# Routing inside a linear-attention and expert block: keys and queries of four groups as two ScalarE parts added by GpSimd, ten groups of base moves on ScalarE, and TensorE's third group ahead of the class counts

## The chip, the cores and the metric

One core of one Trainium2 chip. The metric is the device time of one execution in microseconds (us). TensorE is PE in the profile, VectorE DVE, ScalarE ACT, GpSimd POOL, and SP the queue that starts most transfers.

## What is computed

`x` is (8, 1024, 128). `xn` is its layer norm. The result is `x + attention(xn) + ffn(xn)`, and ffn returns `xn` plus the expert part.

```python
# linear attention, B=8, T=1024, D=128
xn = layer_norm(x, ln_g, ln_b)
q, k, v = split(xn @ qkv_w + qkv_b)
k = k * sigmoid(xn @ gate_w + gate_b)
q = elu(q) + 1.0
k = elu(k) + 1.0
attn = einsum('btd,bsd->bts', q, k) * tril
out = einsum('bts,bsd->btd', attn, v) / (sum(q * cumsum(k)) + DEN_EPS)
# experts, E=8, FF=256, K=2
scores = (x @ router_w.T + router_b) / temp
gates = sinkhorn(scores, iters=3)
topk_vals, topk_idx = top_k(gates, 2)
g = relu(x @ wg[e]);  p = x @ wp[e];  y = (g * p) @ wo[e]
result = x + weighted sum of the two chosen experts
```

## The kernel before, in words

The 8192 tokens are 64 tiles of 128, in 16 groups of four tiles; two groups are one sequence of the batch. Each engine has one instruction stream, written out by hand, and counts on semaphores order them. Nothing is scheduled by a program: an engine does its list in order, and a wait holds all that stands behind it.

Stage one (to about 42 us): statistics, normalised rows, their transposes `zT`, and for each group the logits and values `lv`. At the same time SP clears two scratch arrays in HBM, `by_lower` and `by_upper`.

Stage two, the routing with the first groups of the attention (42 to about 90 us). VectorE runs the Sinkhorn rounds over all tokens: `spread_maxima`, `shift_columns` (then a second exponential on ScalarE, L726, `rB<-rA`), `weigh_rows` (L1019), column sums on TensorE (`route_sums`, L1524), `column_factors` (L1024), `row_factors`, three times; then `first_best`, `second_best` (from L1045), `members` (the last, L1057, makes the class membership), `tile_sums`, `class_bounds`, `slots` (L1084 writes `placed`, the step PLACED). TensorE counts in `route_counts`, `route_totals` and `route_places`. Between these stand the steps of groups 0 to 3. GpSimd meanwhile moves the base rows of all 16 groups (L522: `rows = rows * r1p + base_off`, 64 operations), and then prepares the gates (from L534).

A group n of the attention takes these steps:

- TensorE `project(n, "g")`, `"k"`, `"q"` (L1453): 128x512 products for the gate, the key and the query.
- ScalarE `tanh_gate` (L678), VectorE `gate_key` (L935, tile `kg`), ScalarE `exp_key` (L690, `ek`) and `relu_key` (L693, `rk`), VectorE `key` (L946): `kp = min(ek, 1) + rk`.
- ScalarE `exp_query` (L684, `eq`), VectorE `query` (L941): `qp = max(min(eq, 1), q)` with q read from PSUM.
- TensorE `score(n)` (L1571), VectorE `mask(n)` (L959); TensorE `turn_key(n)` (L1579), ScalarE `save_kt` (L699, `ktok`).
- TensorE `add_state` (L1507) and ScalarE `save_state` (L709) in turn for four tiles; TensorE `out_chunk` (L1491, L1494).
- VectorE `finish(n)` (L965 to L973): divides and adds to the base row. It waits for the base move of its group.

`score(3)` waits for the step PLACED, since the places and the scores share a PSUM bank. On TensorE 34 small filler products (L1620) stand before the counts.

Stage three (to about 170 us): groups 3 to 15 in a loop over `range(EARLY, NG)`, with `EARLY = 3`; GpSimd scatters finished rows to `by_lower` (L557), once the slots are known. ScalarE also splits expert weights after some groups (`round_expert`, L713). Stage four: two passes of 41 entries over the experts, TensorE nearly always busy.

The key and the query on VectorE before are:

```python
def key(n):
    dve.wait_ge(ek_done, n + 1)
    dve.scalar_tensor_tensor(kp[:, n % 2].rearrange("p g t -> p (g t)"), ek[:], 1.0, rk[:],
                             ALU.min, ALU.add).then_inc(kp_done, 1)
```

## Time and profile before

| | us |
|---|---|
| median of 3 runs | 378.62 (378.27 to 380.6) |
| the profiled execution | 379.69 |
| its span in the profile | 376.5 |
| TensorE busy / VectorE busy in the span | 338.0 / 267.9 |
| GpSimd busy / ScalarE busy | 267.7 / 235.8 |

The span is the time between the first and the last instruction that the profiler saw; the rest lies around it. Busy times overlap and can't be added. A timeline row gives the start, the length, the engine, the line, and in square brackets the idle time ahead of it and what ended it.

### The profile page before, as it was taken

What the parts mean: (1) busy time and instruction counts of PE and PEld (TensorE: products, weight loads), DVE (VectorE), ACT (ScalarE), POOL (GpSimd) and SP (SyncE); (2) the same over time, 40 slices, a digit from 0 to 9 for tenths busy, and PEclk for the clock granted to TensorE, in tenths of its full rate; (3) what the DMA queues carried; (4) which work ended last, traced back from release to release, by engine and by line L of the source; (5) the groups of instructions that cost most, each with busy time, mean ns of one, the idle gap of its engine ahead of it and who ended that gap; (6) DMA issues with size and microseconds to landing.
All of it is one profiled execution on the core that took longest, in us unless ns stands there. A gap on an engine that the chain in (4) does not pass through costs nothing.

```text
span 376.5 us, 8784 instructions
## 1 busy us (share of the span) xinstructions
PE 338.0 (90%) x2584; PEld 307.0 (82%) x2584; DVE 267.9 (71%) x733; ACT 235.8 (63%) x442; POOL 267.7 (71%) x363
## 2 busy tenths in 40 slices
PE   0889799889999999988699999999899999999780
PEld 0769568667888887878699999999899999999670
DVE  3998889998888888776545677666666667666440
ACT  3689744225776766657445877777587777775430
POOL 3686999947777756566377677777737777777773
PEclk9999999979999999999989999999999999999996
DMA  6999999998424413248965776776664555553330
GB/s 180 286 326 334 336 334 262 305 265 252 142 103 141 157 71 128 90 140 219 317 209 173 189 220 195 214 219 193 179 172 131 162 143 136 169 150 103 110 87 0
DMA packets 64284, 70.96 MB, mean 188 GB/s; under 512 B 6098, under 2 KB 59102, under 8 KB 64240
## 3 DMA queue, kind: packets, MB, share of 16 engines
q1 hardware_dynamic: 54112, 48.70, 48.8%
q0 software_dynamic: 8672, 21.19, 15.6%
q10 hardware_dynamic: 1456, 0.53, 0.7%
q8 instruction: 22, 0.36, 0.4%
q14 instruction: 22, 0.18, 0.2%
HBM read 28.54 MB, written 43.04 MB: 190 GB/s over the span
## 4 chain that ended last, share of the span: by engine, by line
PE 64%; DVE 13%; DMA 10%; issue 4%; POOL 4%; ACT 2%; SPq 0%; ACTq 0%; DVEq 0%; POOLq 0%
PE psum L1698 13%; PE psum L1683 7%; PE psum L1685 7%; PE psum L1684 7%; PE psum L1507 4%; PE psum L1571 4%; PE psum L1659 3%; DMA row<-by_lower 3%; POOL out L587 3%; PE psum L1400 3%; DVE stats L876 3%; PE psum L1453 2%; PE psum L1491 2%; DMA rows<-in_L_attn_x 2%; DMA by_lower<-rows,slot_u 2%
## 5 line engine op out<-in xcount | busy, mean ns | idle before, releaser
L573 POOL DMA_INDIRECT by_upper<-row x70 | 69.1, 987 | 30.1 <-issue 20.5
L587 POOL DMA_INDIRECT out<-row x70 | 68.9, 985 | 25.9 <-issue 16.5
L557 POOL DMA_INDIRECT by_lower<-rows,slot_u x64 | 63.9, 998 | 30.6 <-issue 17.9
L1698 PE MATMUL psum<-w_expert,hT 128*128 x560 | 77.0, 277 | 0.8 <-DVE hT L1333 0.5
L1683 PE MATMUL psum<-xT_high,w_now 128*128 128x256 f32 x232 | 70.6, 305 | 1.9 <-DVE xT_low L1324 1.1
L1698 PEld LDWEIGHTS psum<-w_expert,hT 128*128 128x128 f32 x560 | 69.7, 192 | 1.5 <-issue 1.1
L788 ACT ACTIVATE w_now<-w_split 128x1024 fp32r x58 | 61.4, 1058 | 14.1 <-PE psum L1685 13.6
L1685 PE MATMUL psum<-xT_high,w_now 128*128 128x256 f32 x232 | 65.7, 283 | 0.0
L1684 PE MATMUL psum<-xT_low,w_now 128*128 128x256 f32 x232 | 65.3, 282 | 0.0
L1337 DVE TENSOR_TENSOR hT<-relu,psum 128x512 f32<-128x512 f32 x58 | 39.9, 688 | 34.7 <-PE psum L1685 30.9
L1345 DVE SCALAR_TENSOR_TENSOR row<-psum,row 128x128 f32<-128x128 f32 x140 | 43.7, 346 | 9.7 <-PE psum L1698 2.8
L807 ACT ACTIVATE relu<-psum 128x512 f32<-128x512 f32 x58 | 34.7, 598 | 20.1 <-PE psum L1685 19.7
L1683 PEld LDWEIGHTS psum<-xT_high,w_now 128*128 128x128 f32 x232 | 44.4, 191 | 2.5 <-ACT w_now L788 1.3
L1684 PEld LDWEIGHTS psum<-xT_low,w_now 128*128 128x128 f32 x232 | 44.4, 191 | 0.0
L1685 PEld LDWEIGHTS psum<-xT_high,w_now 128*128 128x128 f32 x232 | 44.1, 190 | 0.0
L522 POOL TENSOR_SCALAR rows<-rows,r1p,base_off 128x128 f32<-128x128 f32 x64 | 35.1, 564 | 0.1
L1659 PE MATMUL psum<-ident,row 128*128 128x128 f32 x140 | 28.9, 276 | 6.8 <-DMA row<-by_lower 3.6
L1324 DVE TENSOR_TENSOR xT_low<-psum,xT_high 128x256 fp32r<-128x256 f32 x58 | 24.5, 425 | 8.0 <-ACT xT_high L797 4.4
L1507 PEld LDWEIGHTS psum<-lv,ktok 128*128 128x128 f32 x112 | 17.8, 190 | 14.8 <-ACT ktok L699 7.7
L1507 PE MATMUL psum<-lv,ktok 128*128 128x129 f32 x112 | 26.0, 314 | 1.9 <-ACT state L709 0.9
L1673 PE MATMUL psum<-xT_plain,w_plain 128*128 128x128 f32 x192 | 25.4, 275 | 0.0
L1659 PEld LDWEIGHTS psum<-ident,row 128*128 128x128 f32 x140 | 17.9, 142 | 8.3 <-DMA row<-by_lower 4.0
(265 smaller groups left out, 688.0 us busy)
## 6 DMA issues: line engine op xcount, KB each, us to landing
by_lower<-blank SPq DMA_DIRECT2D x1, 10140.0 KB, 34.6
by_upper<-blank SPq DMA_DIRECT2D x1, 10062.0 KB, 71.3
row<-by_lower SPq DMA_DIRECT2D x29, 260.0 KB, 3.6
row<-by_upper SPq DMA_DIRECT2D x29, 258.0 KB, 2.9
rows<-in_L_attn_x SPq DMA_DIRECT2D x8, 512.0 KB, 9.2
row<-by_lower SPq DMA_DIRECT2D x12, 130.0 KB, 3.2
row<-by_upper SPq DMA_DIRECT2D x12, 129.0 KB, 2.2
by_upper<-row POOLq DMA_INDIRECT x70
```

The costliest lines, as they stand in the source:

```text
L557: pool.indirect_dma_start(by_lower, bass.IndirectOffsetOnAxis(ap=slot_u[:, t:t + 1], axis=0), rows[:, t, :], None)\
L573: pool.indirect_dma_start(by_upper, bass.IndirectOffsetOnAxis(ap=row[:, q, k, SLOT_UP:SLOT_UP + 1].bitcast(U32), axis=0), row[:, q, k, 0:R ...
L587: pool.indirect_dma_start(out_rows, bass.IndirectOffsetOnAxis(ap=row[:, q, k, TOKEN:TOKEN + 1].bitcast(U32), axis=0), row[:, q, k, BASE], ...
L788: act.activation(w_now[:, n % 2, :], w_split[:, bass.ds(number, 1), 0:4 * FF].rearrange("p a f -> p (a f)"), ACT.Copy).then_inc(w_copied, 1)
L1337: dve.tensor_tensor(hT[:, n % 3].rearrange("p f t -> p (f t)"), relu[:, n % 2], psum[:, 2 * (n % 2) + 1, :], ALU.mult).then_inc(h_done, 1)
L1345: dve.scalar_tensor_tensor(target, psum[:, 4 + n % 2, k * D:(k + 1) * D], row[:, n % NB, k, by:by + 1], target, ALU.mult, ALU.add)\
L1507: pe.matmul(psum[:, 5, 0:D1], ktok[:, c, :], lv[:, n * G + c, V1], start=(cb == 0), stop=True, skip_group_check=True).then_inc(s_ready, 1)
L1659: last = pe.transpose(psum[:, 6 + n % 2, k * P:(k + 1) * P], row[:, n % NB, k, Z], ident[:])
L1683: pe.matmul(target, high, x_high, start=True, stop=False)
L1684: pe.matmul(target, high, x_low, start=False, stop=False)
L1685: last = pe.matmul(target, low, x_high, start=False, stop=True)
L1698: last = pe.matmul(psum[:, 4 + n % 2, k * D:(k + 1) * D], hT[:, n % 3, f, k * P:(k + 1) * P], weights, start=(f == 0), stop=(f == FB - 1))
```

## The change

Four things change.

- Keys and queries of groups 0 to 3 (`ON_POOL = EARLY + 1`) are no longer made by VectorE. ScalarE makes two parts: `relu(-x)`, `relu(x)` and then `exp(-relu(-x))` of the first; GpSimd adds the two. For the query a new tile `rq` holds the second part. A key takes three ScalarE operations instead of two, a query three instead of one. A semaphore `below` makes the exponential wait for its own input. Groups from 4 on stay as they were.
- Base moves: GpSimd keeps groups 5 to 10, interleaved with its keys and queries. ScalarE takes ten: 0 to 4 among its early steps, and 11 to 15 after groups 5, 7, 9, 11 and 12 (`LATE_BASE`). `base_done` becomes `base_act` and `base_pool`, and `finish` waits for the one that counts its group.
- VectorE's order: keys and queries leave it; `gate_key(2)` moves ahead of `weigh_rows(2)`; `mask(2)`, `gate_key(3)` and `finish(1)` move between the best and the second-best expert; `finish(2)` comes before the slots.
- TensorE's order: the outputs of group 2, the query of group 3 and the gate of group 4 move ahead of the counts, and the 34 filler products go.

The diff, cut to its core:

```diff
+        ON_POOL = EARLY + 1
+        ACT_BASE, POOL_BASE = (0, 1, 2, 3, 4, 11, 12, 13, 14, 15), (5, 6, 7, 8, 9, 10)
...
+        LATE_BASE = {5: 11, 7: 12, 9: 13, 11: 14, 12: 15}
...
-            for n in range(NG):
+
+            def move_base(n):
                 for t in range(n * G, (n + 1) * G):
                     last = pool.tensor_scalar(rows[:, t, BASE], rows[:, t, BASE], r1p[:, t:t + 1],
                                               base_off[:, t:t + 1], ALU.mult, ALU.add)
-                last.then_inc(base_done, 1)
+                last.then_inc(base_pool, 1)
+
+            def query(n):
+                pool.wait_ge(eq_done, n + 1)
+                if n >= 2:
+                    pool.wait_ge(o_ready, n - 1)
+                pool.tensor_tensor(qp[:, n % 2].rearrange("p g t -> p (g t)"), eq[:], rq[:], ALU.add).then_inc(qp_done, 1)
+
+            def key(n):
+                pool.wait_ge(ek_done, n + 1)
+                pool.tensor_tensor(kp[:, n % 2].rearrange("p g t -> p (g t)"), ek[:], rk[:], ALU.add).then_inc(kp_done, 1)
+
+            move_base(5)
+            move_base(6)
+            move_base(7)
+            key(0)
+            query(0)
+            move_base(8)
+            key(1)
+            query(1)
+            move_base(9)
+            key(2)
+            query(2)
+            move_base(10)
+            key(3)
+            query(3)
...
+                if n < ON_POOL:
+                    act.activation(eq[:], psum[:, bank_q(n), :], ACT.Relu, bias=ones[:, 0:1], scale=-1.0).then_inc(below, 1)
+                    act.activation(rq[:], psum[:, bank_q(n), :], ACT.Relu, bias=minus_one[:])
+                    act.wait_ge(below, 2 * n + 2)
+                    act.activation(eq[:], eq[:], ACT.Exp, scale=-1.0).then_inc(eq_done, 1)
+                    return
...
+                if n < ON_POOL:
+                    act.activation(ek[:], kg[:], ACT.Relu, scale=-1.0).then_inc(below, 1)
+                    act.activation(rk[:], kg[:], ACT.Relu)
+                    act.wait_ge(below, 2 * n + 1)
+                    act.activation(ek[:], ek[:], ACT.Exp, scale=-1.0).then_inc(ek_done, 1)
+                    return
...
+                for t in range(n * G, (n + 1) * G):
+                    last = act.activation(rows[:, t, BASE], rows[:, t, BASE], ACT.Identity, bias=base_off[:, t:t + 1],
+                                          scale=r1p[:, t:t + 1])
+                last.then_inc(base_act, 1)
...
+                if n in LATE_BASE:
+                    move_base(LATE_BASE[n])
...
             for n in range(EARLY, NG):
-                finish(n - 1)
+                if n > EARLY:
+                    finish(n - 1)
...
             for n in range(EARLY, NG):
                 ahead = n + 1 < NG
-                if ahead:
+                if ahead and n > EARLY:
                     project(n + 1, "g")
```

Lines of the changed kernel are numbered anew: L726 is L782 there, L1045 is L1110, L1453 is L1512, L1571 is L1630, L1507 is L1566, L1491 and L1494 are L1550 and L1553.

ScalarE, from the first exponential of the routing to the saved key of group 0. Before (`rB<-rA` are the two exponentials, `ek` and `rk` the key's parts, `eq` the query's, `th` the gate):

```order
L721 ACTIVATE rB<-rA 128x512
L690 ACTIVATE ek<-kg 128x512
L693 ACTIVATE rk<-kg 128x512
L684 ACTIVATE eq<-psum,minus_one 128x512
L726 ACTIVATE rB<-rA 128x512
L678 ACTIVATE th<-psum 128x512
L729 ACTIVATE w_high<-w_in 128x384
L690 ACTIVATE ek<-kg 128x512
L693 ACTIVATE rk<-kg 128x512
L684 ACTIVATE eq<-psum,minus_one 128x512
L699 ACTIVATE ktok<-psum 128x512
```

The same place now (the `rows` operations are base moves):

```order
L727 ACTIVATE ek<-kg 128x512
L728 ACTIVATE rk<-kg 128x512
L730 ACTIVATE ek<-ek 128x512
L715 ACTIVATE eq<-psum,ones 128x512
L716 ACTIVATE rq<-psum,minus_one 128x512
L718 ACTIVATE eq<-eq 128x512
L770 ACTIVATE rows<-rows,base_off,r1p 128x128 x4
L782 ACTIVATE rB<-rA 128x512
L708 ACTIVATE th<-psum 128x512
L785 ACTIVATE w_high<-w_in 128x384
```

Between the two exponentials there stood three operations, now ten; between the second one and the saved key the same again, with base move 1 in it.

VectorE now, around the second-best expert (`scores` is the mask of group 2, `kg` the gated key of group 3, `den` to `rows` the finish of group 1, `rA<-rank,score` the start of the second best):

```order
L1103 TENSOR_REDUCE score<-best_h 128x64
L1018 TENSOR_TENSOR scores<-psum,causal 128x512
L994 SCALAR_TENSOR_TENSOR kg<-th,psum 128x512
L1030 TENSOR_SCALAR den<-psum 128x4
L1033 RECIPROCAL rden<-den 128x4
L1038 SCALAR_TENSOR_TENSOR rows<-psum,rden,rows 128x128 x4
L1110 TENSOR_TENSOR rA<-rank,score 128x512
```

Before, the mask and the gated key stood behind the members, and query 3 and the reciprocal of the gates behind the finish:

```order
L1057 TENSOR_TENSOR member<-cls,class_no 128x896
L959 TENSOR_TENSOR scores<-psum,causal 128x512
L1064 CAST tile_sum<-psum 64x14
L935 SCALAR_TENSOR_TENSOR kg<-th,psum 128x512
```

The mask of group 2 and the gated key of group 3 have moved ahead of the second best, and with them the finish of group 1.

## Rows read from the trace of the kernel before

**Rows 1.** The page, busy time by engine: us, share of the span, instructions

```profile
PE 338.0 (90%) x2584; PEld 307.0 (82%) x2584; DVE 267.9 (71%) x733; ACT 235.8 (63%) x442; POOL 267.7 (71%) x363
```

**Rows 2.** Busy time of each engine by stretch, granted clock, DMA

```profile
core 0: us, PE busy (x) PEld busy (x) DVE busy (x) ACT busy (x) POOL busy (x), PEclk, DMA share, GB/s
...
60.00:70.00 10.00, 8.93 (x65) 7.48 (x64) 9.62 (x20) 4.04 (x9) 10.00 (x18) 1.00 1.07 251
...
80.00:90.00 10.00, 10.00 (x47) 7.36 (x45) 8.65 (x25) 2.49 (x6) 5.30 (x9) 0.68 1.09 275
```

**Rows 3.** Timeline of TensorE, scores of groups 3, 4 and 5

```profile
86.03 1.24 PE L1571 MATMUL psum<-qp,kp 128*128 128x128 f32 x8
...
93.05 1.16 PE L1571 MATMUL psum<-qp,kp 128*128 128x128 f32 x8
...
99.78 1.05 PE L1571 MATMUL psum<-qp,kp 128*128 128x128 f32 x8
```

**Rows 4.** Timeline of ScalarE: four normalised tiles; key 0, query 0, second exponential

```profile
13.26 1.64 ACT L620 ACTIVATE rows<-rows,z_off,rs 128x128 f32<-128x128 f32 x4
...
45.22 0.63 ACT L690 ACTIVATE ek<-kg 128x512 f32<-128x512 f32 x1 [0.48 <-DVE kg L935]
...
45.76 0.61 ACT L693 ACTIVATE rk<-kg 128x512 f32<-128x512 f32 x1
...
46.41 0.69 ACT L684 ACTIVATE eq<-psum,minus_one 128x512 f32<-128x512 f32 x1
...
48.28 0.63 ACT L726 ACTIVATE rB<-rA 128x512 f32<-128x512 f32 x1 [1.19 <-DVE rA L1013]
```

**Rows 5.** Timeline of GpSimd and VectorE where both work on 128x64 or 128x384

```profile
23.38 1.00 POOL L487 TENSOR_TENSOR w_in<-w_in,w_sum 128x384 f32<-128x384 f32 x1
...
73.78 0.72 POOL L534 TENSOR_TENSOR rC<-rC 128x256 f32<-128x256 f32 x1
73.91 0.64 DVE L1055 TENSOR_SCALAR cls<-v 128x64 f32<-128x64 f32 x1
74.47 0.18 DVE L1056 TENSOR_SCALAR cls<-u 128x64 f32<-128x64 f32 x1
...
74.69 1.24 DVE L1057 TENSOR_TENSOR member<-cls,class_no 128x896 bf16<-128x896 f32 x1
75.06 1.04 POOL L536 TENSOR_TENSOR score<-score 128x64 f32<-128x64 f32 x1
```

**Rows 6.** Timeline: first row weights, column sums of rounds 1 and 2, third column factors

```profile
48.94 0.69 DVE L1019 TENSOR_TENSOR rC<-rB,u 128x512 f32<-128x512 f32 x1
...
55.33 2.00 PE L1524 MATMUL psum<-rC,ones 128*128 128x64 f32 x16
...
61.20 1.90 PE L1524 MATMUL psum<-rC,ones 128*128 128x64 f32 x16
...
63.72 0.55 DVE L1024 RECIPROCAL v<-psum 128x64 f32<-128x64 f32 x1
```

**Rows 7.** Timeline of TensorE: query of group 2, last output product of group 1

```profile
63.38 1.88 PE L1453 MATMUL psum<-zT,w_in 128*128 128x512 f32 x4
...
67.97 0.39 PE L1494 MATMUL psum<-state,qp 128*128 128x129 f32 x2
```

**Rows 8.** Timeline of VectorE: second best, mask of group 2, places

```profile
69.11 0.68 DVE L1045 TENSOR_TENSOR rA<-rank,score 128x512 f32<-128x512 f32 x1
...
75.96 0.69 DVE L959 TENSOR_TENSOR scores<-psum,causal 128x512 f32<-128x512 f32 x1
...
80.83 1.97 DVE L1084 TENSOR_TENSOR placed<-psum,member 128x448 f32<-128x448 f32 x2
```

**Rows 9.** Timeline of ScalarE, group 5 in the loop

```profile
106.22 0.60 ACT L678 ACTIVATE th<-psum 128x512 f32<-128x512 f32 x1 [0.81 <-PE psum L1456]
107.89 0.60 ACT L699 ACTIVATE ktok<-psum 128x512 f32<-128x512 f32 x1 [1.07 <-PE psum L1579]
```

**Rows 10.** GpSimd's waits: engine, line, waited for, us in total, times, longest

```profile
POOL by_lower L557 <- DVE rows L973: 12.3, 12, 2.0
```

**Rows 11.** Busy time by engine and granted clock in one us

```profile
85.00:86.00 1.00, 1.00 (x2) 0.34 (x1) 0.93 (x6) 0.00 (x0) 0.69 (x1) 0.50 1.14 262
```

More of the change, by code:

```diff
@@ L241, in sparse_block_kernel @@
             eq = first("eq", [P, GW])
+            rq = first("rq", [P, GW])
             kp = first("kp", [P, 2, G, P])
@@ L261, in sparse_block_kernel @@
             "rw_loaded rw_pe rw_step w_scaled w_summed w_sum_saved w_step")
-        (stat_step, var_ready, sqrt_out, scale_ready, z_act, z_dve, z_pool, zT_ready, zT_act, zT_dve, base_done) = steps(
-            "stat_step var_ready sqrt_out scale_ready z_act z_dve z_pool zT_ready zT_act zT_dve base_done")
+        (stat_step, var_ready, sqrt_out, scale_ready, z_act, z_dve, z_pool, zT_ready, zT_act, zT_dve, base_act, base_pool, below) = steps(
+            "stat_step var_ready sqrt_out scale_ready z_act z_dve z_pool zT_ready zT_act zT_dve base_act base_pool below")
         lv_ready = [sem(f"lv_ready{g}") for g in range(NG)]
@@ L717, in round_z, with move_base @@
                 act.activation(z_high(n), group(n), ACT.Copy).then_inc(z_rounded, 1)
+            def move_base(n):
+                if n == 0:
+                    act.wait_ge(scale_ready, len(BLOCKS) + 1)
+                    act.wait_ge(z_act, len(ACT_Z))
+                    act.wait_ge(z_dve, len(DVE_Z))
+                    act.wait_ge(z_pool, len(POOL_Z))
+                for t in range(n * G, (n + 1) * G):
+                    last = act.activation(rows[:, t, BASE], rows[:, t, BASE], ACT.Identity, bias=base_off[:, t:t + 1],
+                                          scale=r1p[:, t:t + 1])
+                last.then_inc(base_act, 1)
             tanh_gate(0)
@@ L739, in _ @@
             exp_key(2)
-            relu_key(2)
             save_kt(1)
@@ L746, in _ @@
             save_state(1, 2)
+            move_base(3)
+            exp_key(3)
             save_kt(2)
@@ L960, in mask, with wait_base @@
                                   causal[:].unsqueeze(1).to_broadcast([P, G, P]), ALU.mult).then_inc(a_masked, 1)
+            def wait_base(n):
+                if n in ACT_BASE:
+                    dve.wait_ge(base_act, ACT_BASE.index(n) + 1)
+                else:
+                    dve.wait_ge(base_pool, POOL_BASE.index(n) + 1)
             def finish(n):
@@ L1136, in _ @@
             shift_columns()
-            query(0)
             weigh_rows(0)
-            key(0)
             gate_key(1)
@@ L1144, in _ @@
             mask(0)
-            query(1)
-            key(1)
             column_factors(1)
             row_factors()
+            gate_key(2)
             weigh_rows(2)
-            gate_key(2)
             mask(1)
@@ L1154, in _ @@
             first_best()
-            query(2)
-            key(2)
+            mask(2)
+            gate_key(3)
+            finish(1)
             second_best()
             members()
-            mask(2)
             tile_sums()
-            gate_key(3)
             class_bounds()
-            finish(1)
-            query(3)
+            finish(2)
             invert_gates()
             slots()
-            key(3)
             def pair_bounds():
@@ L1617, in _ @@
             add_state(2, 1)
+            out_chunk(2, 0)
+            out_chunk(2, 1)
+            project(3, "q")
             add_state(2, 2)
-            for _ in range(34):
-                pe.matmul(psum[:, ROUTE_BANK, 0:P], before_h[:], before_h[:], start=True, stop=True)
+            out_chunk(2, 2)
+            add_state(2, 3)
+            out_chunk(2, 3)
+            project(4, "g")
             route_counts()
             route_totals()
-            project(3, "q")
             route_places()
-            add_state(2, 3)
-            for c in range(G):
-                out_chunk(2, c)
             for n in range(EARLY, NG):
                 ahead = n + 1 < NG
-                if ahead:
+                if ahead and n > EARLY:
                     project(n + 1, "g")
```

15 lines of the change are left out of this document (9 added, 6 removed).

## The prediction, made before the changed kernel ran

> **What bounds the kernel now.** I began with the share of time by engine: TensorE is busy 90% of the span and VectorE 71% [rows 1], an average over stages with different limits. So I cut the span into stretches [rows 2]. From 60 to 70 us VectorE is busy 96%, from 80 to 90 us 87%, TensorE's weight loads 75 and 74% and ScalarE 40 and 25%: this is the routing, from 42 to 85 us, one long chain on VectorE (exponential, three rounds of row and column factors, best and second-best expert, classes, places), and the first four groups of the linear attention are woven into it. From 100 us on the groups run alone at an even pace: their scores start at 86.03, 93.05 and 99.78, 6.7 us apart [rows 3]. Each group depends on the states of the last, and the expert stage needs the last rows, so whatever moves the score of group 4 (93.05) moves everything behind it. All groups from 4 on keep their instructions; only five groups' base moves on ScalarE are new there. So the whole question is when the score of group 4 starts.
>
> The profiled execution took 379.69 us: 376.5 of span and 3.2 around it. The median of the runs is 378.62. I work out a difference in the trace and add it to the median.
>
> **The step units.** ScalarE: the two passes over the key start 0.54 apart (45.22, 45.76), and a pass that reads PSUM with a bias takes 0.69, about 0.60 from start to start; a 128x128 pass with scale and bias costs 1.64 for four, that is 0.385 each and 1.54 for a group [rows 4]. So a key in parts takes 3 x 0.54 = 1.62 where it took 1.08, a query 0.60 + 0.60 + 0.54 = 1.74 where it took 0.60. Four groups: 4 x (0.54 + 1.14) = 6.7 us more, and ten base moves 15.4 us, five of them (7.7 us) before group 3. GpSimd: the addition of two 128x512 tensors isn't in the trace. The nearest row is 1.00 for 128x384, the same operation [rows 5]: from below 1.0, from above 1.0 x 512/384 = 1.33 plus what a neighbour on VectorE may add (1.7); I take 1.35. VectorE loses eight operations of 0.69, which start 0.60 apart: 4.8 us.
>
> **The change, leg by leg**, against the trace of before. A time of the new kernel is a sum of row durations along its written order.
>
> 1. *To the first row weights.* The second exponential ran at 48.28 on ScalarE, as soon as VectorE had its input [rows 4]. Now it stands behind key 0 (45.22 + 1.62), query 0 (+ 1.74) and base move 0 (+ 1.54): 50.1. The first row weights, at 48.94 before, start at 50.75: **+1.8**. Before, VectorE's query 0 ran beside the exponential; nothing covers the wait now.
>
> 2. *To the second column sums.* TensorE's column sums of round 1 are queued behind the first state product, which needs the saved key of group 0. On ScalarE that save is now behind gate 1, key 1 (from 52.3, 1.62), base move 1 (1.54), query 1 (1.74): it ends at 57.8, and the sums start at 58.0 where they started at 55.33 [rows 6]: +2.6 in all, **+0.8** on this leg. That VectorE reaches the same place at 57.3 or, if GpSimd's additions don't hold it, at 56.2, changes nothing: ScalarE is late.
>
> 3. *To the third column factors.* Sums end 60.1; reciprocal, factors, sum and reciprocal 2.6; the gate of key 2 is now written ahead of the row weights (0.60); weights 0.70 and sums 2.0: the factors of round 3 start at 66.1. Before it was 63.72, where the sums were done at 63.1 and waited for VectorE's mask and finish [rows 6]: +2.4 in all, **-0.2**. Removing queries and keys from VectorE pays here, little.
>
> 4. *To the second-best expert.* This is the worst place. The best expert takes 4.0 us, to 70.1. Then the mask of group 2 is written, which needs its scores. Before, TensorE began that group's query at 63.38 and was through its queue (last product of group 1 at 67.97, 0.22 to the next) at 68.2 [rows 7], 4.8 us later; the mask stood 7 us further down VectorE's order (75.96) and never waited. Now the query's product starts after the third sums and four transposes, at 66.35; 4.8 more and 0.8 for states that ScalarE saves only after the three parts of query 2 and gate 3: scores start 72.0, are out at 73.2. VectorE stands still 3.1 us. Gate 3 then waits for its key product, which is behind scores (0.89), transposes (0.46) and its own 1.05: 74.4, another 0.6. Mask and gate 1.2, finish of group 1 1.45. Second best starts at 76.5, where it was 69.11 [rows 8]: +7.4 in all, **+5.0**.
>
> 5. *Second best and class members.* 69.11 to 75.93 before, 6.8. The same operations now run beside key 3 and query 3 on GpSimd. What that costs: a 128x64 step on the class numbers took 0.64 beside GpSimd's addition and ended with it (74.55 and 74.50), the next one took 0.18; and GpSimd's 128x64 product beside the member test took 1.04, as long as 128x384 elsewhere [rows 5]. So the two hold each other up. Between 0 and 1.9 us (two additions of 1.35, less the part before VectorE comes); I take **+1.3**.
>
> 6. *Members to places.* 75.93 to 82.80 before. The chain is counts 0.64, copy, totals, bounds 0.8, places, a reciprocal, two products of 0.97. Mask, gate and query have left it and the finish of group 2 has come in; 6.65 against 6.87: **-0.2**. Places are known at 91.3.
>
> 7. *Places to the scores of group 3.* Here is the gain. Before, the products of group 2's output, the gate product of group 4 and key 3 came after: the scores started 3.2 us behind the places, at 86.03. Now all that is done, and the scores start at once: **-3.2**.
>
> 8. *Group 3.* 7.02 us before. One finish (1.45) has left VectorE, but slot sums, casts and pair bounds now follow the places there: 7.2, **+0.2**.
>
> Sum: 1.8 + 0.8 - 0.2 + 5.0 + 1.3 - 0.2 - 3.2 + 0.2 = +5.5. Scores of group 4 at 98.5.
>
> **What is hidden.** The five late base moves (1.54 each) are in groups without an expert split or with a free stretch: in group 5 (from 106 us) ScalarE waits 0.81 before the gate and 1.07 behind it [rows 9], 1.88 in all for 1.54. They cost nothing; uncovered they would cost 5 x 1.54 = 7.7 us. GpSimd's scatters start some 7.6 us later but the rows only 5.5; it waited 12.3 us in all for rows [rows 10], and 2.1 us of that go, so it still catches up before the last group. The expert stage is untouched.
>
> **A rule weighed.** The rows above show GpSimd and VectorE holding each other up [rows 5]. The Trainium skill, "SBUF — State Buffer" (SBUF: two separate sides), says that the two share a port pair as "an **exclusive lock**, not a bandwidth split", taken by an operation of VectorE with two SBUF inputs against a GpSimd operation that reads SBUF. The trace agrees in both pairs of leg 5. By the rule in full, leg 5 is +1.9, without it 0: a total of +6.1 or +4.2.
>
> **The rivals.**
> *A, the clock.* TensorE's granted clock averages 0.68 from 80 to 90 us [rows 2] and stands at 0.50, its level of 1.2 GHz, at 85 [rows 11], after a stretch with waits for the members; the 34 filler products are gone now, and TensorE is idle from 74.4 to 77.4 and for much of 84 to 91. If the half clock comes later and reaches into group 3 (it doubles some 3 to 4 us of products there and in the places), the total is +8 to +9: 387. For it: the stalls of leg 4. Against: more products stand before the counts. Chance 0.2.
> *B, half of it.* ScalarE's and TensorE's delays overlap better: no hold-up by GpSimd (-1.3), scores of group 2 not behind the states (-0.8), the half clock, which lay on the path of legs 6 and 7, gone (-1): +2.4, 381. Chance 0.2.
> *C, faster.* VectorE was 87 to 96% busy [rows 2]: if the chain stays bound by it and GpSimd and ScalarE keep ahead, eight operations (4.8) leave it and leg 7 comes in full with 3.2, less 1.8 of leg 1 and the 1.3 of leg 5: -4.9, 373.7. Its place is the mask of group 2: it decides if scores 2 are out by 70.1, that is 3.1 us sooner than worked out. Against: leg 2 by ScalarE's queue alone. Chance 0.13.
>
> **How the numbers follow.** The forecast (legs as above, +4 to +7) has 0.47. Predicted 378.62 + 5.5 = 384.1 us. The range runs from B's low end, 379.5, to A's 388; outside lie C and a few hundredths. Slower by over 1% (3.8 us, about what a measurement of this kernel tells from no change) is the forecast, A and a little of B: 0.69; within 1%: most of B, 0.18; faster: C, 0.13.
>
> **What would show it.** In the profile after: the second exponential at 50, sums of round 1 at 58, VectorE idle before the mask of group 2 by about 3 us with TensorE's scores as the releaser, second best at 76 to 77, the scores of group 3 right behind the places near 91, group 4 at 98 to 99, then 6.7 a group. If the mask of group 2 doesn't wait, leg 4 and the sign are wrong; if the scores of group 4 come later than 100, look at the granted clock from 80 to 98; if the pace after group 4 isn't 6.7, the late base moves weren't hidden.

## The result, and the profile after

| | before | after |
|---|---|---|
| median of 4 runs, us | 378.96 (378.27 to 380.6) | 385.36 (381.94 to 386.64) |
| profiled execution / its span | 379.69 / 376.5 | 384.35 / 382.6 |
| start of the second exponential | 48.28 | 50.00 |
| second-best expert starts | 69.11 | 76.28 |
| class members known / places known | 75.93 / 82.80 | 83.24 / 91.97 |
| scores of group 3 / group 4 | 86.03 / 93.05 | 92.23 / 101.90 |

The changed kernel is slower: ratio 1.017, with a 95% interval from 1.0121 to 1.022. The forecast was 384.1 us, a difference of 5.5 where 6.4 was measured. The sign and the place are right. Three terms of the sum are not: together they put the scores of group 4 at 8.85 us late instead of 5.5, and part of that comes back at the end of the kernel.

The page of after, busy time by engine, answers to [rows 1]:

```profile
PE 337.8 (88%) x2550; PEld 306.7 (80%) x2550; DVE 263.3 (69%) x725; ACT 256.0 (67%) x494; POOL 254.8 (67%) x331
```

VectorE has lost 4.6 us of work and GpSimd 12.9, ScalarE has gained 20.2. VectorE was the busiest engine of the routing, and the kernel is slower all the same. The waits of VectorE say why. View: waits of VectorE in after, 50 to 100 us (what waited, what it waited for, us in total, times, longest):

```profile
DVE scores L1018 <- PE psum L1630: 4.1, 2, 3.1
DVE tile_sum L1129 <- PE psum L1591: 2.8, 1, 2.8
DVE v L1089 <- PE psum L1583: 2.8, 2, 1.4
DVE rC L1084 <- ACT rB L782: 2.6, 1, 2.6
```

Each line is a wait: 2.6 us for the second exponential, 3.1 for the scores of group 2, 2.8 for the counts. The 4.6 us that VectorE no longer works it waits, and more. The same three places in the timeline of VectorE in after (start, length, line, idle time ahead and its releaser):

```profile
50.73 0.69 DVE L1084 TENSOR_TENSOR rC<-rB,u 128x512 f32<-128x512 f32 x1 [2.59 <-ACT rB L782]
...
72.94 0.69 DVE L1018 TENSOR_TENSOR scores<-psum,causal 128x512 f32<-128x512 f32 x1 [3.13 <-PE psum L1630]
74.23 0.69 DVE L994 SCALAR_TENSOR_TENSOR kg<-th,psum 128x512 f32<-128x512 f32 x1 [0.60 <-PE psum L1512]
...
76.28 0.68 DVE L1110 TENSOR_TENSOR rA<-rank,score 128x512 f32<-128x512 f32 x1
...
86.08 0.16 DVE L1129 CAST tile_sum<-psum 64x14 bf16<-64x14 f32 x1 [2.84 <-PE psum L1591]
```

They answer to [rows 6] and [rows 8]. TensorE's granted clock is the last piece. View: TensorE by stretches of 2 us in after (stretch, us, busy us and count, granted clock, DMA share, GB/s):

```profile
78.00:80.00 2.00, 1.99 (x9) 0.50 1.11 243
80.00:82.00 2.00, 2.00 (x9) 0.68 1.10 262
82.00:84.00 2.00, 0.63 (x6) 1.00 1.14 246
...
86.00:88.00 2.00, 0.78 (x10) 1.00 1.01 315
88.00:90.00 2.00, 1.98 (x13) 0.53 0.40 123
90.00:92.00 2.00, 0.00 (x0) 0.50 0.03 11
92.00:94.00 2.00, 1.77 (x8) 0.50 0.00 0
94.00:96.00 2.00, 2.00 (x8) 0.50 0.00 0
96.00:98.00 2.00, 2.00 (x5) 0.50 0.37 133
98.00:100.00 2.00, 2.00 (x14) 0.92 0.19 67
```

The clock is at 0.50, its level of 1.2 GHz, from 78 to about 81 and again from 88 to 98 us, the second time right through group 3. TensorE had stood idle for 3.02 us up to 77.15 before the first fall, and was busy only 0.63 us from 82 to 84 and 0.78 from 86 to 88 before the second.

### The profile page after: what moved, and what is told of

The parts are those of the page before. It is cut to its first block, busy times and chain, and to the rows that moved or that the text cites. A ratio compares the mean times of both kernels' runs of the same rounds, so it can differ in the third digit from the quotient of the medians.

```text
span 382.6 us, 8732 instructions
## 1 busy us (share of the span) xinstructions
PE 337.8 (88%) x2550; PEld 306.7 (80%) x2550; DVE 263.3 (69%) x725; ACT 256.0 (67%) x494; POOL 254.8 (67%) x331
## 4 chain that ended last, share of the span: by engine, by line
PE 69%; DVE 8%; ACT 6%; DMA 6%; issue 5%; POOL 4%; SPq 0%; ACTq 0%; DVEq 0%; POOLq 0%
PE psum L1758 14%; PE psum L1743 7%; PE psum L1745 7%; PE psum L1744 7%; PE psum L1566 5%; PE psum L1630 4%; PE psum L1733 4%; PE psum L1719 4%; POOL out L617 3%; PE psum L1459 3%; PE psum L1550 2%; PE psum L1512 2%; DVE stats L935 2%; PE psum L1553 2%; DMA rows<-in_L_attn_x 2%
## 5 line engine op out<-in xcount | busy, mean ns | idle before, releaser
L587 POOL DMA_INDIRECT by_lower<-rows,slot_u x64 | 65.0, 1015 | 29.4 <-issue 18.5
L1566 PEld LDWEIGHTS psum<-lv,ktok 128*128 128x128 f32 x112 | 18.5, 195 | 22.1 <-ACT ktok L743 11.8
L1566 PE MATMUL psum<-lv,ktok 128*128 128x129 f32 x112 | 26.1, 315 | 7.8 <-ACT ktok L743 4.8
L1550 PE MATMUL psum<-lv,scores 128*128 128x129 f32 x128 | 24.0, 280 | 0.0
```

What stands on the lines that cost most here:

```text
L587: pool.indirect_dma_start(by_lower, bass.IndirectOffsetOnAxis(ap=slot_u[:, t:t + 1], axis=0), rows[:, t, :], None)\
L1566: pe.matmul(psum[:, 5, 0:D1], ktok[:, c, :], lv[:, n * G + c, V1], start=(cb == 0), stop=True, skip_group_check=True).then_inc(s_ready, 1)
```

## The experiments

The start of the routing moves by 2 us between executions. So from here on a point is counted from the column shift, one VectorE operation that stands ahead of all that changes (47.56 in before, 47.45 in after, 46.2 to 48.3 in the others). All in us behind it:

| kernel | first row weights | column sums, round 1 | second best | members | places | scores 3 | scores 4 | ratio to before, 95% |
|---|---|---|---|---|---|---|---|---|
| before | 1.38 | 7.77 | 21.55 | 28.37 | 35.24 | 38.47 | 45.49 | 1 |
| after | 3.28 | 10.51 | 28.83 | 35.79 | 44.52 | 44.78 | 54.45 | 1.017, 1.012 to 1.022 |
| x1 | 1.74 | 9.87 | 28.64 | 36.56 | 43.63 | 43.88 | 52.99 | 1.016, 1.010 to 1.023 |
| x2 | 3.28 | 14.11 | 32.43 | 39.39 | 48.55 | 48.81 | 56.18 | 1.022, 1.017 to 1.028 |
| x3 | 3.28 | 13.10 | 31.41 | 39.33 | 45.71 | 46.61 | 53.38 | 1.013, 1.006 to 1.021 |
| x4 | 3.28 | 13.68 | 25.56 | 32.12 | 45.60 | 45.86 | 55.25 | 1.028, 1.024 to 1.033 |
| x5 | 3.29 | 10.53 | 28.85 | 35.81 | 44.34 | 44.60 | 53.91 | 1.020, 1.014 to 1.026 |
| x6 | 3.28 | 10.52 | 28.83 | 36.74 | 45.51 | 46.15 | 54.25 | 1.020, 1.012 to 1.028 |
| x7 | 3.27 | 10.52 | 22.40 | 29.60 | 36.97 | 37.61 | 45.57 | 0.996, 0.992 to 1.001 |
| x8 | 1.39 | 7.77 | 21.54 | 28.35 | 35.66 | 35.92 | 44.10 | 0.998, 0.994 to 1.001 |
| x9 | 3.29 | 14.11 | 25.99 | 33.19 | 40.57 | 41.20 | 49.17 | 1.000, 0.995 to 1.005 |
| x10 | 1.75 | 9.57 | 21.46 | 28.66 | 36.05 | 36.67 | 44.62 | 0.989, 0.983 to 0.996 |
| x11 | 3.28 | 10.53 | 28.84 | 35.51 | 43.80 | 46.40 | 53.12 | 1.015, 1.010 to 1.021 |
| x12 | 1.75 | 9.57 | 21.46 | 28.66 | 36.05 | 36.67 | 44.63 | 0.995, 0.990 to 1.001 |

Read the table by differences in a row, not only by its last time. Each row is one profiled execution; where the clock is the same, a step repeats to a few hundredths. The ratio is against the kernel before in the same job. Filler products compute nothing that is used: they only keep TensorE busy.

### x1: early base moves back on GpSimd

```diff
-        ACT_BASE, POOL_BASE = (0, 1, 2, 3, 4, 11, 12, 13, 14, 15), (5, 6, 7, 8, 9, 10)
+        ACT_BASE, POOL_BASE = (11, 12, 13, 14, 15), tuple(range(11))
```

> The changed kernel with base moves 0 to 4 on GpSimd (as before the change) instead of ScalarE, the late ones 11 to 15 still on ScalarE. Theory Q (each leg is set by a queue, and the loss at the second-best expert is by the keys and queries in parts): the second exponential comes 1.5 us earlier (48.5 instead of 50.0), the row weights of round 1 at 49.2, the column sums of round 1 at about 56 instead of 57.96; but GpSimd now has the moves ahead of its additions, the scores of group 2 come hardly earlier (71 to 72), second best at 75 to 76.5, scores of group 4 at 100 to 102: total 383.5 to 386, within 1% of the changed kernel. Rival S (ScalarE's five early base moves, 7.7 us, carry the loss): scores of group 4 at 96 or before, total 379 to 380.

Median 384.68. The row weights come 1.54 us sooner, one base move exactly, but the column sums only 0.64, and second best 0.19. So the five early moves (7.7 us of ScalarE's time) aren't the loss. (At the scores of group 4 this profile is 1.46 us ahead of after; in the ratio nothing of it shows.) Leg 1 was won and lost again at the next wait: the key product of group 1 waited 1.58 us for GpSimd's query 0, and gate 1 waited 0.84 for it.

### x2: the counts ahead of two states

```diff
             project(3, "q")
+            route_counts()
+            route_totals()
             add_state(2, 2)
...
-            project(4, "g")
-            route_counts()
-            route_totals()
             route_places()
+            project(4, "g")
```

> The changed kernel with TensorE's class counts and totals written behind query 3's product, ahead of the states (2,2), (2,3) and their outputs, and the gate product of group 4 behind the places. Theory Q (in the changed kernel the counts, at 85.37, stand in TensorE's queue behind states that ScalarE saves only after query 3 in three parts): the counts start right behind the tile sums' copy, at 82.9 to 83.5, the idle time of 2.84 before the tile sum on VectorE falls to about 1, places known at 89.5 to 90.5 instead of 91.97; the gate product of group 4 then stands between places and scores 3 and takes 0.9 to 1.7 back: scores 3 at 91 to 92, scores 4 at 100.5 to 101.9, total 383.5 to 385.5. Rival C (only the half clock, which products in the queue merely stretch, matters): the places come at 91.5 or later, as the same products fall into the same stretch at 0.50.

The counts started 0.06 us behind the members (86.45 against 86.39) where after needs 2.13, as theory Q has it. But from members to places it took 9.16 us, no less than after's 8.73: TensorE ran at 0.50 from 80 to 96 us, and states, outputs and places stretched. So up to the places the new order pays nothing while the clock is down. Behind them it does: from scores 3 to scores 4 it took 7.37 us instead of 9.67, the clock being back at 1.00 from about 97 us, and from the second best to scores 4 it took 23.75 instead of 25.62. Both expectations of this run hold in half. And a new thing shows: the clock was at 0.50 already at 50 us, and the column sums came at 14.11 instead of 10.51. These 3.6 us hide the gain in the time.

### x3: 119 fillers in the tail

```diff
+            pe.wait_ge(a_masked, 3)
+            keep_warm(50, ROUTE_BANK)
             add_state(2, 0)
...
+            keep_warm(20, 3)
             add_state(2, 3)
...
             route_totals()
+            keep_warm(15, 3)
             route_places()
+            keep_warm(34, 3)
```

> The changed kernel with 119 filler products on TensorE, in its idle stretches of the routing's tail: 50 behind the masked scores of group 2 (74 to 77 us), 20 and 15 about the counts, 34 behind the places' product. They compute nothing that is used. Theory C (the half clock from 78 to 98 costs 2.5 us in group 3 and 0.5 to 1 before the places): granted clock near 1.0 from 78 to 98, places at 91 to 91.5, scores 3 to scores 4 in 7.0 to 7.3 us instead of 9.67, scores 4 at 98 to 99, total 381 to 382.5. Rival W (group 3 is long because slot sums, casts and bounds on VectorE stand in its way, whatever the clock): the clock rises but scores 3 to scores 4 stays at 9 us or more, total 384 to 386.

View: TensorE in x3, by 2 us, about the counts and the places (members at 87.11, places at 93.49):

```profile
84.00:86.00 2.00, 1.74 (x21) 1.00 1.06 319
86.00:88.00 2.00, 1.39 (x16) 1.00 0.51 157
88.00:90.00 2.00, 1.90 (x26) 1.00 0.08 19
90.00:92.00 2.00, 2.00 (x16) 0.57 0.00 0
92.00:94.00 2.00, 2.00 (x24) 0.58 0.00 0
94.00:96.00 2.00, 2.00 (x23) 1.00 0.00 0
```

Scores 3 to scores 4 took 6.77 us instead of 9.67, members to places 6.38 instead of 8.73. Rival W is out: the missed part of leg 8 is the clock. The fillers cost 0.6 of it back, since the last 34, partly at half clock, ended 0.9 us behind the places.

TensorE's order is that of after here, and still the counts start 0.06 us behind the members. View: timelines of GpSimd, VectorE and TensorE in x3:

```profile
84.84 1.32 POOL L535 TENSOR_TENSOR qp<-eq,rq 128x512 f32<-128x512 f32 x1 [3.84 <-ACT eq L718]
85.07 2.04 DVE L1122 TENSOR_TENSOR member<-cls,class_no 128x896 bf16<-128x896 f32 x1
87.17 0.60 PE L1591 MATMUL psum<-ones_h,member 128*64 128x1 bf16 x14 [0.39 <-DVE member L1122]
```

Of that, 0.95 us is the members themselves, which end later (2.04 us beside GpSimd's query 3 instead of 1.09). The rest of after's 2.13 is the same queue run through at the full clock. From the second best to scores 4 it took 21.97 us instead of 25.62, so holding the clock up in the tail is worth 3.65, and it pays alone. The median is 383.30, but the ratio, 1.013 against 1.017, has an interval that overlaps after's: the early fall of the clock was in this profile too, with 2.59 us at the column sums.

### x4: the tail's orders as before

The orders of VectorE, TensorE and ScalarE from the second-best expert on are those of before; keys, queries and base moves stay where the change put them.

```diff
-            mask(2)
-            gate_key(3)
-            finish(1)
             second_best()
             members()
+            mask(2)
             tile_sums()
+            gate_key(3)
             class_bounds()
-            finish(2)
+            finish(1)
```

> The changed kernel, keys and queries still in three ScalarE parts added by GpSimd and base moves on ScalarE, but the orders of VectorE, TensorE (with its 34 filler products) and ScalarE from the second-best expert on as in the kernel before. Theory Q: the mask of group 2 no longer stands ahead of the second-best expert, which starts at 70.5 to 72 instead of 76.28; the class members end at 76 to 77.5 instead of 83.24; the price comes later: key 3 and query 3 on GpSimd and the outputs of group 2 behind the places, scores 4 at 97 to 100, total 379 to 383, between the two kernels. Rival P (the parts and GpSimd's additions are themselves too slow, wherever the mask stands): second best starts no earlier than 74 or the members' steps beside GpSimd take over 8 us, scores 4 at 101.5 or later, total 385 or more.

The slowest of all, 388.32. Second best came 3.27 us sooner than in after although the column sums were 3.17 later: 6.44 in all, the two waits for scores and key product (3.13 and 0.60) and the work of mask, gate and finish. And then it was thrown away. View: VectorE's timeline in x4, ahead of the places:

```profile
84.14 1.13 DVE L1038 SCALAR_TENSOR_TENSOR rows<-psum,rden,rows 128x128 f32<-128x128 f32 x4
91.03 0.55 DVE L1144 RECIPROCAL score<-score 128x64 f32<-128x64 f32 x1 [5.76 <-POOL score L571]
91.50 1.90 DVE L1149 TENSOR_TENSOR placed<-psum,member 128x448 f32<-128x448 f32 x2
```

VectorE stood 5.76 us for GpSimd's gate sums. View: GpSimd in x4:

```profile
84.82 1.27 POOL L539 TENSOR_TENSOR kp<-ek,rk 128x512 f32<-128x512 f32 x1 [7.87 <-ACT ek L730]
86.48 1.27 POOL L535 TENSOR_TENSOR qp<-eq,rq 128x512 f32<-128x512 f32 x1 [0.40 <-ACT eq L718]
87.71 0.73 POOL L564 TENSOR_TENSOR rC<-rC 128x256 f32<-128x256 f32 x1
```

GpSimd had waited 7.87 us for key 3 with the gates queued behind it, and their input was ready at 78.3. I had expected 97 to 100 for scores 4, and neither theory named this wait.

### x5: fillers in the early gaps

```diff
             project(1, "g")
+            warm(26)
             project(1, "k")
+            warm(6)
             route_sums(0)
...
+            warm(18)
             add_state(0, 0)
```

> The changed kernel with 50 filler products on TensorE in the gaps that the parts leave in group 0: 26 ahead of the key product of group 1 (TensorE stood idle 1.57 us there, with GpSimd's query 0 as the releaser), 6 more ahead of the column sums of round 0, 18 ahead of the first state product. They compute nothing that is used. Theory E (new, from the three profiles in which the clock stood at 0.50 between 48 and 59 us: the gap that the query in parts opens at 48 to 50 us lets the clock fall in some executions, which costs 3 us before the column sums of round 1 and lies in the changed kernel's median): clock 1.0 from 48 to 60, column sums of round 1 at 57.5 to 58.5 in every execution, median 1.5 to 3 us below the changed kernel's 385.4, at 382.5 to 384, no execution over 385.5. Rival N (the early half clock is chance that has nothing to do with the gap, or the fillers delay as much as they save): median within 1 us of 385.4, or executions at 386 to 387 as before.

The clock stood at 1.00 from 40 to 70 us and the sums at 10.53, and the runs drew together (385.61 to 386.49). But the median is 386.01 and the ratio 1.020, no lower than after's. So the profiles show an early fall in four of the six kernels that have the gap without fillers or a mended front (x2, x3, x4, x9, not after and x1) and in none of the six that have those, yet that it lies in after's median isn't shown. Theory E fell in its time.

### x6: early and late fillers, counts first

```diff
             project(3, "q")
+            warm(40, 3)
             route_counts()
+            warm(6, 3)
             route_totals()
+            warm(6, 3)
             add_state(2, 2)
```

> The changed kernel with three things at once: the early fillers, fillers in the tail (50 behind the masked scores of group 2, 40 ahead of the counts, 20 about the totals and the gate product) and the counts ahead of the states (2,2), (2,3). Theory: at the full clock the counts start within 0.2 us of the members (83.2), the places are out at 89.5 to 90.3 (91.97 in the changed kernel), scores 3 at 90 to 91, scores 4 at 97 to 98 (101.90), total 379.5 to 381.5. Rival W (VectorE's steps on the totals and GpSimd's gates, not TensorE, set the places): places at 91.5 or later at the full clock, scores 4 at 98.5 to 99.5, total 382 to 383.

The cut shows the late ones; the early fillers of x5 and 50 more behind the masked scores, as in x3, stand ahead of them.

Missed: 385.71. The counts started 0.06 us behind the members, but these took 0.95 longer (the last of their steps 2.03 us beside GpSimd's query 3 instead of 1.09). The 40 fillers ran out at 81.7, TensorE was idle 1.98 us, the clock was at 0.50 from about 86 to 96, and the places came at 45.51. That fillers have to reach to the next work is what this run and x11 suggest (there 4.94 us idle behind the fillers, then half clock); no run tries it alone.

### x7: x4 with the gates ahead of key 3 and query 3

```diff
             move_base(10)
-            key(3)
-            query(3)
...
+            key(3)
+            query(3)
             pool.wait_ge(gates_inverted, 1)
```

with the early fillers of x5.

> The kernel of x4 (orders of the tail as before the change), with GpSimd's first ten gate steps written ahead of key 3 and query 3, and the early fillers. In x4 VectorE stood still 5.76 us before it could invert the gates, since GpSimd's gates stood behind query 3. Theory Q (that queue alone cost x4 its gain): the invert comes at 81 to 83, places out at 85 to 87, scores 3 at 87 to 89, scores 4 at 94 to 96.5, total 379 to 381, within 1% of the kernel before. Rival L (GpSimd's additions beside VectorE's steps hold both up): the steps from second best to members take 8 us instead of 6.5 and the gates 5 us instead of 4, places at 89 or later, total 383 or more.

Median of ten runs 377.30, the same as before's 377.30 in that job, ratio 0.996 with 1 just inside the interval; scores 4 at 45.57, before 45.49. That is better than expected. VectorE waited 0.20 us ahead of the places, and the clock was at 1.00 in every stretch to 105 us. The hold-ups of rival L are half there (second best to members 7.20 us, gate steps 5.0) but the places don't wait for them.

### x8: the kernel before, key 3 sooner and 20 more fillers

```diff
-            slots()
             key(3)
+            slots()
...
+            warm(6)
             route_counts()
+            warm(6)
             route_totals()
+            warm(8)
             project(3, "q")
```

> The kernel before the change, with key 3 on VectorE ahead of the places instead of behind the slots, and 20 more filler products (6 ahead of the counts, 6 and 8 about the totals). Theory: the clock, 0.50 from 80 to 87 us before, stays at 1.0, TensorE is through the gate product of group 4 at 83.2 instead of 86.2, and the scores of group 3 start behind the places, at 83.4 to 84 instead of 86.03; scores 4 at 90.5 to 91; total 375 to 377 against 378.7, that is 1.5 to 2.5 us faster. Rival: the clock falls all the same, or finish 2 and mask 3 on VectorE come later behind the slots and take it back: scores 4 at 92.5 or later, no difference.

The clock stayed at 1.00 from 80 to 90 us (0.68 before, [rows 2]) and scores 3 came 2.55 us sooner. Of that 1.39 were left at scores 4, because VectorE then works from the places to key 4 with one gap of 0.18 us. Median 376.20 against 377.30: ratio 0.998 with 1 inside the interval, no difference that is shown. The rival's point is half right. Key 3's place and the fillers were changed together, so their shares stay open.

### x9: x7 without the early fillers

> The kernel of x7 without its 50 early filler products: x4 with GpSimd's first ten gate steps ahead of key 3 and query 3, nothing else. Times of a point are counted from VectorE's column shift (the subtraction of the column maxima, at 47.45 in the changed kernel, 46.2 to 48.3 in the others), since the start of the routing itself moves by 2 us between executions. Theory G (the gates' place alone is what separates x4 and x7 in the tail): from the column sums of round 1 to the scores of group 4 it takes 35 us as in x7 (35.05) instead of x4's 41.57; total 378 to 382, depending on whether the clock falls at 50 us. Theory E (early fillers matter in x7 too): the profile shows the clock at 0.50 somewhere from 48 to 58 us, the sums at 13 to 14 us behind the shift instead of 10.5, and the median is 2 to 3 us over x7's 377.3. Rival: the median is 377 to 378.5 with sums at 10.5, and the early half clock of x2 to x4 was chance that costs the median nothing.

From the column sums to scores 4 it took 35.06 us, x7 35.05, x4 41.57. So theory G holds to a hundredth: the place of the gate steps in GpSimd's queue is worth 6.5 us. It isn't all wait: from the members to the places 6.10 is saved, behind the places 1.05, where x4 ran at half clock (0.50 from 94 to 98 us) after TensorE's idle 4.92, and the steps from second best to members take 0.64 more. The clock fell at 49 us and the sums were at 14.11, as theory E has it for the profile. View: TensorE's timeline in x9:

```profile
49.28 2.07 PE L1510 MATMUL psum<-zT,w_in 128*128 128x512 f32 x2 [1.57 <-POOL qp L535]
51.15 3.51 PE L1581 MATMUL psum<-rC,ones 128*128 128x64 f32 x16
```

Products take nearly twice their 1.12 and 1.90 us, behind an idle time of 1.57 that GpSimd's query ends. The 2 to 3 us that theory E puts on the median aren't shown: the ratio, 1.000, lies 0.4% above x7's, within both intervals.

In the jobs of x9 to x11 and of x12 every kernel took 65 to 70 us longer than in the others (before: 447.74 and 442.98). View: waits in x10, 92 to 125 us (what waited, what it waited for, us in total, times, longest):

```profile
ACT state L753 <- remote: 8.4, 1, 8.4
```

ScalarE waited 8.4 us with no releaser in the kernel. Up to the scores of group 4 these traces show no such wait, so their columns stand, and of the times only the ratios are used.

### x10 and x12: the front mended

```diff
-            move_base(0)
             act.wait_ge(route_dve, COL_SHIFTED)
...
             exp_key(1)
-            move_base(1)
+            move_base(0)
...
-                        pe.wait_ge(qp_done, n)
+                        pe.wait_ge(eq_done, n)
                     product(psum[:, 1, :], WK)
```

Base moves 1 to 3 go one place later each, and of x7's early fillers (26, 6 and 18) 0, 6 and 14 stay.

> The kernel of x7 with the front mended: base move 0 on ScalarE behind key 1 instead of ahead of the second exponential, base moves 1, 2 and 3 one place later each (3 into ScalarE's 3 us wait for gate 3), and TensorE's key products of groups 1 to 3 waiting for ScalarE's passes over the query's PSUM bank instead of for GpSimd's addition, which doesn't read it; of the early fillers only 6 and 14. Theory Q (legs 1 and 2 are ScalarE's queue): row weights at 1.7 to 1.9 us behind the column shift instead of 3.3, column sums of round 1 at 9.0 to 9.4 instead of 10.5, scores of group 4 at 44.0 to 44.5 instead of 45.57; median 375.5 to 376.5, faster than the kernel before by 0.2 to 0.5%. Rival: GpSimd's additions now lie beside VectorE's steps of the first round and hold them up (a 1.64 step instead of 0.69 twice), sums at 10 or later, median 377 to 378 as x7.

> The kernel of x10 unchanged, once more, since in the job of x9 to x11 every kernel, the one before the change too, took some 70 us longer behind the first groups (ScalarE and TensorE stood still there with nothing in the kernel that held them), which makes their absolute times useless. Theory Q: scores of group 4 at 44.4 to 44.9 us behind the column shift (before 45.49, x7 45.57), median 375.3 to 376.7 against 377.3 to 379 for the kernel before, ratio 0.993 to 0.998. Rival: the ratio of 0.989 in that job was real and holds here too (median 373 to 374.5), or was a matter of that job alone and the ratio here is 1.0.

Row weights at 1.75 as expected; sums at 9.57, 0.2 over the expected end. The rival has a share in that: the first row weights now took 1.28 us beside GpSimd's query 0 (0.70 in x7). Scores 4 at 44.62 and 44.63, 0.87 sooner than before. The ratios are 0.989 and 0.995; the first interval is wholly below 1, the second touches it. By the trace 0.2% is earned; that it is 0.5% or 1% no step explains. So a gain over the kernel before is not shown: x10 has the one interval of twelve runs that lies wholly below 1, and that of its repetition doesn't.

### x11: the mask ahead, alone

x7 with the change's order of VectorE only:

```diff
+            mask(2)
+            gate_key(3)
+            finish(1)
             second_best()
             members()
-            mask(2)
             tile_sums()
-            gate_key(3)
             class_bounds()
-            finish(1)
```

> The kernel of x7 with mask 2, gate 3 and finish 1 on VectorE ahead of the second-best expert, as the change has them; everything else (TensorE's, ScalarE's and GpSimd's order, early fillers) as in x7. It is leg 4 of the forecast alone: VectorE waits about 3.1 us for the scores of group 2 and 0.6 for key 3's product and does 2.65 us of work first, second best starts at 28.5 to 29 us behind the column shift instead of 22.4; of these 6.4 us, 2.65 come back when mask, gate and finish are missing between members and places. Theory Q: places and scores 3 later by 3.5 to 4.5 than in x7, scores 4 at 49 to 50 behind the shift (45.57), median 380.5 to 382. Rival H (in x7 the places are bound by something else, the counts' chain or GpSimd's gates, which hide the wait): scores 4 at 47.5 or before, median below 379.5.

Second best at 28.84, as said, +6.44 against x7; scores 4 at 53.12, +7.55, where 3.5 to 4.5 was expected. View: TensorE in x11, by 4 us:

```profile
78.00:82.00 4.00, 0.00 (x0) 1.00 1.10 268
82.00:86.00 4.00, 3.28 (x19) 0.54 1.08 299
86.00:90.00 4.00, 4.00 (x25) 0.50 0.39 121
```

While VectorE goes through second best and members TensorE is idle 4.94 us, even behind the 34 fillers, and then query 3, the places and the outputs of group 2 run at half clock. VectorE waits 3.29 us ahead of the places. One moved block gives 7.55 of the 8.96 us that the whole change costs at this point. Of these, 6.44 are there at the second best; the expected return of 2.65 us between members and places didn't come, since there VectorE waits for TensorE at half clock.

## Why the prediction was right, and where it was wrong

In short: its queues were right, its clock wasn't, and that the difference came out within 1 us is in part luck. At the scores of group 4 the delay is 8.85 us, which is rival A's "+8 to +9" by rival A's mechanism, given a chance of 0.2; at the end of the kernel 6.4 are left, near the forecast's 5.5.

By its legs, in after against before, in the times of the two profiles:

| leg | predicted | measured |
|---|---|---|
| 1 first row weights | +1.8 | +1.79 |
| 2 second column sums | +0.8 | +0.84 |
| 3 third column factors | -0.2 | -0.45 |
| 4 second best | +5.0 | +4.99 |
| 5 members | +1.3 | +0.14 |
| 6 places | -0.2 | +1.86 |
| 7 scores 3 | -3.2 | -2.97 |
| 8 scores 4 | +0.2 | +2.65 |
| sum | +5.5 | +8.85 |

**Legs 1 to 4 and 7 hold.** A queue followed instruction by instruction gave each within 0.25 us, and x11 shows leg 4 as a cause: +6.44 with everything else held. But leg 1 wasn't the whole of its mechanism. x1 and x10 show that without the base move the next bound is GpSimd's query 0, for which TensorE's key product waits although GpSimd doesn't read the bank. The prediction didn't price that wait.

**Leg 5 was mis-sized**, +1.3 against +0.14. A step of VectorE and an addition of GpSimd held each other, as weighed: VectorE's L1111 took 1.64 us beside key 3 on GpSimd, and 0.69 in x11, where GpSimd was idle. But before had hold-ups of its own with the gate steps [rows 5], and these left: the class step took 0.20 instead of 0.64, the membership 1.09 instead of 1.24. I added the new and didn't take off the old. And of the two additions only key 3 lay there: query 3, late by the half clock, started at 83.50, behind the members. In x3 it lies over the membership test, and leg 5 is +1.10. View: timelines of GpSimd and VectorE in after, a step in the first round that the prediction didn't name, and L1111; then query 3 and the counts:

```profile
53.92 1.27 POOL L539 TENSOR_TENSOR kp<-ek,rk 128x512 f32<-128x512 f32 x1 [1.76 <-ACT ek L730]
54.10 1.64 DVE L1092 TENSOR_TENSOR rC<-rB,v 128x512 f32<-128x512 f32 x1
...
76.70 1.38 POOL L539 TENSOR_TENSOR kp<-ek,rk 128x512 f32<-128x512 f32 x1 [4.65 <-ACT ek L730]
76.99 1.64 DVE L1111 SCALAR_TENSOR_TENSOR rB<-rA,rC 128x512 f32<-128x512 f32 x1
...
83.50 1.27 POOL L535 TENSOR_TENSOR qp<-eq,rq 128x512 f32<-128x512 f32 x1 [5.42 <-ACT eq L718]
...
85.37 0.60 PE L1591 MATMUL psum<-ones_h,member 128*64 128x1 bf16 x14
```

The first costs nothing there, since ScalarE is late anyway. The Trainium skill, "SBUF — State Buffer" (SBUF: two separate sides), calls this an exclusive lock: an operation of VectorE with two SBUF inputs and one of GpSimd that reads SBUF take turns, and the one that starts first holds the ports for its whole instruction. The trace agrees in both: GpSimd starts 0.18 and 0.29 us ahead, and VectorE's step ends 0.55 us behind GpSimd's end, where alone it takes 0.69. One of the two pairs from which the prediction read the rule, the class step `cls<-v` of [rows 5], has a single tensor input, so it isn't a case of the rule as it was put there; the membership test is.

**Leg 6 had the wrong sign**, and the failed step is "Mask, gate and query have left it". It looked at VectorE's list alone. TensorE's list ahead of the counts had grown by states that ScalarE saves only behind query 3 in three parts, at half clock from 78 to 81 us, and the counts started 2.13 us behind the members. Either remedy brings them to 0.06: the counts first (x2), or the same list at the full clock (x3, where the members too end 0.95 later). But only with the clock up do the places come sooner: 14.30 us behind the second best in x3, 15.69 in after, 16.12 in x2.

**Leg 8 was mis-sized**, +0.2 against +2.65, and it is rival A's mechanism: the half clock reached into group 3. x3 measures it, 6.77 against 9.67. I had given it 0.2 because more products stood ahead of the counts; they were done too early to cover the wait.

**Legs 5 to 8 together** show how much of the miss is the clock. The forecast had -1.9 for them. Measured from the second best to the scores of group 4 it is +1.68 in after (25.62 against 23.94) and -1.97 in x3 (leg by leg +1.10, -0.49, -2.33, -0.25). With the clock mostly up the forecast's queues come out within 0.1 of their number, or 0.6 below it if what the fillers cost is taken off.

**Rival B** needed the opposite, the half clock gone and the scores of group 2 ahead of the states: the clock stayed down longer, and the mask waited its 3.13 us.

**The end gave time back.** The scores of group 4 came 8.85 later and the expert product that waits for the scattered rows 8.47 (197.10 against 188.63), but TensorE's last product 7.34 (374.29 against 366.95) and GpSimd's last write 6.13 (376.33 against 370.20); the span grew by 6.1, the profiled time by 4.66 and the median by 6.4. So by the traces the time comes back in the expert stage, 1.2 of it where the last writes follow the last products. No run tries why. The prediction carried its sum to the end unchanged, so its 384.1 is nearer than its working, and that is luck. The pace behind group 4 was 6.6 where 6.7 was said, so the late base moves are hidden.

**Rival C** had its place right. With the mask out of the way (x7) it takes 11.88 us from the column sums of round 1 to second best, before 13.78: 1.90 of VectorE's eight operations come through. But the sums themselves come 2.75 late, by ScalarE's queue, and at scores 4 nothing is left (45.57 against 45.49).

## What to carry to other kernels

When work leaves the busiest engine, follow the list of every engine that takes it, and every block moved ahead of the critical operation for its wait; here mask, gate and finish written ahead of the second best cost 7.55. Put work that others wait for (the gate steps, 3.3 us up to the one waited for) ahead of an operation whose input comes late: its place in a queue was worth 6.5 us. Count an idle TensorE twice, as the wait and as the half clock behind it: here the second cost 3.65 us, as much as the forecast missed at the scores of group 4 (3.35).

## What the hardware showed that I had not expected

- With the same instructions up to there, the granted clock fell to 0.50 in four profiles (x4 at 48.0 us, x9 at 49.0, x2 at 49.2, x3 at 52.6) and not in a fifth (after). TensorE was idle for at most 1.57 us at a time there, and in x4 the clock fell ahead of that idle time, so that gap can't be the cause there; no profile with fillers in it shows the fall. It cost 2.6 to 3.6 us at the column sums.
- A GpSimd addition of two 128x512 tensors takes 1.27 us alone and up to 1.73 beside steps of VectorE; the forecast took 1.35.
- With the same kernel, some jobs ran 65 to 70 us longer, in the four traces from them all of it behind the scores of group 4, with waits of up to 8.7 us (x11, ScalarE) that no instruction of the kernel ended. Why stays open.
